# A second, channel-major copy of x in place of TensorE transposes, with the first norm's scale and shift read back as rows from DRAM

## The reference

```python
def layernorm(x):                       # over the 256 channels
    return (x - mean(x)) / sqrt(var(x) + 1e-5)
def attn(x):                            # RWKV time mixing
    x_prev = x shifted by one token
    xk, xv, xr = (x * m + x_prev * (1 - m) for m in (mix_k, mix_v, mix_r))
    k, v, r = xk @ W_k.T, xv @ W_v.T, sigmoid(xr @ W_r.T)
    return (r * wkv_scan(k, v, decay, first)) @ W_o.T      # a scan over tokens
def ffn(x):                             # ternary weights w, scales s
    h = silu(x @ w1.T * s1) * (x @ w2.T * s2)              # 256 -> 1024
    h = gelu(h @ h1.T * sh1); h = gelu(h @ h2.T * sh2)     # 1024 -> 1024, twice
    return h @ w3.T * s3                                   # 1024 -> 256
x = x + attn(layernorm(x)); x = x + ffn(layernorm(x))
```

## Time and profile before

| | |
|---|---|
| median of 3 runs | 1482.69 us (1480.98 to 1483.41) |
| the profiled execution | 1483.14 us, its span 1481.4 us |
| busy share of the span | PE 99%, PEld 90%, DVE 74%, ACT 70%, POOL 6% |
| chain that ended last | PE 98%, ACT 1%, DVE 1% |
| granted TensorE clock | 1.00 throughout |

### The profile page before, as it was taken

The page is one execution under the profiler, slowest core; times in us unless marked ns, Lnnn a source line. Parts: engine busy times, 40 slices in busy tenths (PEclk is TensorE's granted clock), DMA queues, the critical chain, the costliest instruction groups (busy, mean ns, idle before and its releaser), DMA issues.

```text
span 1481.4 us, 28040 instructions
## 1 busy us (share of the span) xinstructions
PE 1471.6 (99%) x10348; PEld 1328.8 (90%) x10348; DVE 1100.9 (74%) x1519; ACT 1040.1 (70%) x1637; POOL 93.2 (6%) x125
## 2 busy tenths in 40 slices
PE   8999999999999999999999999999999999999998
PEld 7989898998989989898898989989899898998998
DVE  6786878768687686877858777686876868778565
ACT  7995775777667676676867767776677766768655
POOL 1112000010000101001010000100001000010000
PEclk9999999999999999999999999999999999999999
DMA  9987573745737467364564746557374673746653
GB/s 353 382 293 240 171 237 104 237 131 199 233 97 252 114 205 216 124 230 135 204 184 155 229 112 228 154 179 240 100 238 120 212 220 107 250 117 205 178 191 124
DMA packets 95070, 285.28 MB, mean 193 GB/s; under 512 B 9152, under 2 KB 33344, under 8 KB 93248
## 3 DMA queue, kind: packets, MB, share of 16 engines
q1 hardware_dynamic: 86880, 277.01, 55.4%
q0 software_dynamic: 8160, 7.87, 4.3%
HBM read 250.76 MB, written 33.03 MB: 192 GB/s over the span
## 4 chain that ended last, share of the span: by engine, by line
PE 98%; ACT 1%; DVE 1%; issue 0%; POOL 0%; POOLq 0%; DVEq 0%; ACTq 0%
PE acc L674 27%; PE acc L676 26%; PE att L567 10%; PE acc L649 7%; PE acc L648 7%; PE acc L700 4%; PE acc L702 4%; PE att L606 3%; PE att L546 2%; PE acc L803 2%; PE acc L805 2%; PE att L649 1%; PE att L648 1%; PE acc L774 1%; PE acc L543 0%; ACT early L1209 0%
## 5 line engine op out<-in xcount | busy, mean ns | idle before, releaser
L674 PE MATMUL acc<-op_hi,ring 128*128 128x256 f32 x3360 | 810.9, 286 | 0.5 <-issue 0.5
L676 PE MATMUL acc<-op_lo,ring 128*128 128x256 f32 x3360 | 789.0, 278 | 0.0
L674 PEld LDWEIGHTS acc<-op_hi,ring 128*128 128x128 f32 x3360 | 632.1, 188 | 18.7 <-issue 17.6
L676 PEld LDWEIGHTS acc<-op_lo,ring 128*128 128x128 f32 x3360 | 631.1, 188 | 11.1 <-issue 10.0
L1654 DVE TENSOR_TENSOR op_lo<-blocks,op_hi 128x1024 fp32r<-128x1024 f32 (+2 forms) x271 | 339.7, 1268 | 110.7 <-ACT op_hi L1074 104.0
L1074 ACT ACTIVATE op_hi<-blocks 128x1024 fp32r<-128x1024 f32 (+2 forms) x263 | 284.1, 1092 | 81.3 <-DVE blocks L1649 75.0
L648 PE MATMUL acc<-x_hi,w_rnd 128*128 128x512 f32 x420 | 167.3, 398 | 0.0
L649 PE MATMUL acc<-x_lo,w_rnd 128*128 128x512 f32 x420 | 166.1, 396 | 0.0
L1114 ACT ACTIVATE blocks<-acc,vec 128x256 f32<-128x256 f32 x268 | 104.8, 476 | 68.3 <-PE acc L676 60.8
L1114 ACT ACTIVATE blocks<-parts,vec 128x256 f32<-128x256 f32 x240 | 101.1, 497 | 64.1 <-DVE parts L1712 61.5
L700 PE MATMUL acc<-w_rnd,op_hi 128*128 128x256 f32 x504 | 121.9, 284 | 0.0
(11 more groups left out here) (206 smaller groups left out, 1919.9 us busy)
## 6 DMA issues: line engine op xcount, KB each, us to landing
ring<-scratch SPq DMA_DIRECT2D x426, 512.0 KB, 4.2
scratch<-stage SPq DMA_DIRECT2D x11, 1024.0 KB, 12.6
stage<-in_w_ffn SPq DMA_DIRECT2D x10, 1024.0 KB, 10.6
x_in<-in_x SPq DMA_DIRECT2D x32, 256.0 KB, 4.7
out<-x_next SPq DMA_DIRECT2D x30, 256.0 KB, 4.9
out<-mix_v POOLq DMA_DIRECT2D x30, 256.0 KB, 4.3
scratch<-in_w_ffn SPq DMA_DIRECT2D x4, 1024.0 KB, 14.7
ring<-stage SPq DMA_DIRECT2D x7, 512.0 KB, 10.9
```

The source lines that it names most:

```text
L674: pe.matmul(out, act(w), act(op_hi[:, k, c, :]), start=(begins and c == 0 and m % 2 == 0), stop=False, skip_group_check=True)
L676: mm = pe.matmul(out, act(w), act(op_lo[:, k, c, :]), start=False, stop=(c == QC - 1), skip_group_check=True)
```

## The change

It affects tiles 2 to 15 (the loop's mixing).

- The host lays out a second copy of x by channel, x_T. SP loads a tile of it (load_xT, 512 KB in runs of 1 KB) into mix_r, which is free at the end of the iteration.
- DVE takes the statistics of tile i + 2 one iteration earlier, near the end of iteration i (next_statistics), and load_x moves from the end of SP's iteration to behind the 20th refill, where x_in is free.
- POOL makes scale and shift of them (next_deviation). Since in channel order each token is a column, they must lie along the row of every partition: spread_norm stores the 1024 numbers to DRAM in token order, waits for the store, and reads the 4 KB row back to all 128 partitions of norm, once transpose_x2 has read norm.
- POOL applies them: normal_x, a multiply and an add of 128x1024 each, from mix_r and norm into seq, at the head of its iteration.
- transpose_x, ln1 and copy_x leave the loop; the gate has no transposes within. carry_on, two copies of 128x4 that hand on the last token, moves from ACT to DVE, and DVE's mixing waits there for normal_x.
- On DVE lo01(1), prod(7), lo23(1) and lo45(1) stand earlier, on ACT hi23(1).

```diff
@@ SP
+            def load_xT(t):
+                sp.wait_ge(WHOLE.pe_kvr.sem, WHOLE.pe_kvr.at(t - 1))
+                stand_alone(sp, spare, t)
+                ld_xT.add(sp.dma_start(mix_r[:].rearrange("p c (n t) -> p (c n) t", n=n_seq), xT_tiles[:, :, t, :]))
+
+            def spread_norm(t):
+
+                sp.wait_ge(pool_rstd.sem, pool_rstd.at(t - 1, 1))
+                stand_alone(sp, spare, t)
+                st_norm.add(sp.dma_start(norm_rows.rearrange("a (k b p) -> p (a k) b", k=2, p=P), next_norm[:], allow_slow_non_contiguous=True))
+                sp.wait_ge(st_norm.sem, st_norm.at(t))
+                stand_alone(sp, spare, t)
+                sp.wait_ge(WHOLE.pe_x2T.sem, WHOLE.pe_x2T.at(t - 1))
+                stand_alone(sp, spare, t)
+                ld_norm.add(sp.dma_start(norm[:], norm_rows.broadcast_to([P, 2 * TILE])))
...
             with sp.Fori(1, NT - 2) as i:
-                refill(i)
-                load_x(i + 2)
+                refill(i, more_x=True)
                 keep_x1(i + 1)
+                load_xT(i + 2)
+                spread_norm(i + 2)
                 stored(i)
@@ TensorE, the loop
-                    gate(i, range(HC - 1))
-                    pe.wait_ge(dve_prod.sem, dve_prod.at(i, 3))
-                    transpose_x(WHOLE, i + 1)
-                    gate(i, [HC - 1])
+                    gate(i)
                     step(i, 0, 0)
                     step(i, 0, 1)
+                    pe.wait_ge(dve_prod.sem, dve_prod.at(i, 3))
                     project(WHOLE, i + 1, [0, 1, 2])
@@ ScalarE, the loop
                 silu(i, 4)
-                ln1(WHOLE, i + 1)
                 silu(i, 5)
                 hi01(i, 1)
                 silu(i, 6)
-                copy_x(WHOLE, i + 1)
                 hi45(i, 0)
                 silu(i, 7)
                 hi23(i, 0)
+                hi23(i, 1)
                 hi45(i, 1)
                 copy_kvr(WHOLE, i + 1, [0])
-                hi23(i, 1)
                 p1(i, 0)
@@ VectorE
+            def next_statistics(t):
+
+                dve.wait_ge(ld_x.sem, ld_x.at(t + 1))
+                statistics(WHOLE, t, x_in)
+                variance(WHOLE, t, dve_var.add, next_var, next_mean)
+
+            def carry_on(t):
+
+                link(WHOLE, dve.tensor_copy(seq[:, :, :, 0:1], carry_x[:]))
+                dve.wait_ge(pool_x.sem, pool_x.at(t))
+                settle(WHOLE, t)
+                link(WHOLE, dve.tensor_copy(carry_x[:], seq[:, :, :, SEG:SEG + 1]))
...
                 loG11(i)
+                next_statistics(t)
                 loG21(i)
@@ GpSimd
+            def next_deviation(t):
+                deviation(WHOLE, t, dve_var.sem, dve_var.at(t, 2), pool_rstd.add, (next_var, next_mean), (next_norm[:, 0, :], next_norm[:, 1, :]))
+
+            def normal_x(t):
+
+                pool.wait_ge(ld_xT.sem, ld_xT.at(t))
+                pool.wait_ge(ld_norm.sem, ld_norm.at(t))
+                stand_alone(pool, spare, t)
+                pool_x.add(pool.tensor_tensor(now, by_seq(mix_r[:]), row_scale, ALU.mult))
+                pool.wait_ge(pool_x.sem, pool_x.at(t, 1))
+                pool_x.add(pool.tensor_tensor(now, now, row_shift, ALU.add))
...
             with pool.Fori(1, NT - 1) as i:
-                tile_deviation(i + 1, 1)
+                normal_x(i + 1)
                 tile_deviation(i + 1, 2)
+                next_deviation(i + 1)
                 add_out(i)
```

More of the change, by code:

```diff
@@ L123, in __init__, with build @@
         self.dve_x2 = by_chunk("dve_x2", chunks, like and like.dve_x2)
-def build(nc, x, vectors, w_mix, w_ffn, s3, out):
+def build(nc, x, x_T, vectors, w_mix, w_ffn, s3, out):
     n_seq, T, D = x.shape
@@ L145, in build @@
     USES = HALF_STEPS // SLOTS
+    X_AFTER = 19
+    DVE_EXTRA = 6
     assert vectors.shape[1] == 5 * DC + 4 * HC and w_ffn.shape[1] == 2 * W12 + 2 * HH + W3
@@ L210, in build @@
         offset = sb("offset", [P, NB])
+        next_var = sb("next_var", [P, NB])
+        next_mean = sb("next_mean", [P, NB])
+        next_norm = sb("next_norm", [P, 2, NB])
         zeros = sb("zeros", [P, NB])
@@ L267, in build @@
         scratch = nc.dram_tensor("scratch", [2, STEPS + 1, 2, P, HALF], F32, kind="Internal").ap()
+        norm_rows = nc.dram_tensor("norm_rows", [1, 2 * TILE], F32, kind="Internal").ap()
         w_plain = nc.dram_tensor("w_plain", [P, W3], F32, kind="Internal").ap()
@@ L274, in build @@
         norm_ch = norm[:].rearrange("p (c t) -> p c t", c=DC)
+        row_scale, row_shift = (norm[:, k * TILE:(k + 1) * TILE].rearrange("p (a n t) -> p a n t", a=1, n=n_seq).broadcast_to([P, DC, n_seq, SEG])
+                                for k in range(2))
         out_tok = mix_v[:].rearrange("p c t -> p (c t)").rearrange("p (b d) -> p b d", b=NB)
@@ L334, in build @@
         WHOLE = Mixing(ctx, nc, DC, range(n_seq), HALVES, SEG, [BANK[b] for b in (6, 7, 6, 7)], by_block(norm[:]),
[L335 removed]
+                       Chain(ctx, nc, "dve_chain", 36), Chain(ctx, nc, "pool_chain", 2), ahead=1, seqs_ahead=0, like=FIRST[0])
         pe_a, pe_b, pe_half, pe_w3 = (tally(n, k) for n, k in (("pe_a", HC), ("pe_b", HC), ("pe_half", HALF_STEPS), ("pe_w3", 2)))
@@ L357, in build @@
         ld_x = tally("ld_x", n_seq, 16)
+        ld_xT = tally("ld_xT", 1, 16, ahead=-2)
+        st_norm = tally("st_norm", 1, 16, ahead=-2)
+        ld_norm = tally("ld_norm", 1, 16, ahead=-2)
+        pool_x = tally("pool_x", 2, 1, ahead=-2)
         st_out = tally("st_out", n_seq, 16, ahead=0)
@@ L425, in load_plain, with refill @@
                     sp.dma_start(flat(eighth[l]), src).then_inc(ld_eighth[l], 16)
-            def refill(i, last=False, following=WEIGHTS):
+            def refill(i, last=False, following=WEIGHTS, more_x=False):
                 for n in range(HALF_STEPS - SLOTS if last else HALF_STEPS):
@@ L430, in refill @@
                     load_ring((n + SLOTS) % HALF_STEPS, LAST_WEIGHTS if last else following if n + SLOTS >= HALF_STEPS else WEIGHTS)
+                    if more_x and n == X_AFTER:
+                        load_x(i + 2)
             def refill_plain(l, steps):
@@ L514, in _ @@
             load_x(2)
+            load_xT(2)
             refill_plain(1, range(SLOTS))
             keep_x1(1)
+            spread_norm(2)
             stored(0)
             with sp.Fori(1, NT - 2) as i:
-                refill(i)
-                load_x(i + 2)
+                refill(i, more_x=True)
                 keep_x1(i + 1)
+                load_xT(i + 2)
+                spread_norm(i + 2)
                 stored(i)
+            sp.sem_inc(ld_x.sem, 16 * n_seq)
             refill(NT - 2, following=LAST_WEIGHTS)
@@ L1871, in _ @@
             rest_x2(late_seq, 0)
-            dve.sem_inc(WHOLE.dve_chain.sem, WHOLE.dve_chain.per)
+            WHOLE.dve_chain.n = -DVE_EXTRA
+            dve.sem_inc(WHOLE.dve_chain.sem, WHOLE.dve_chain.per - DVE_EXTRA)
             dve.wait_ge(ld_x.sem, ld_x.at(1))
@@ L1942, in _ @@
                 prod(i, 5)
+                lo01(i, 1)
                 t23(i, 0)
-                lo01(i, 1)
                 prod(i, 6)
+                carry_on(t)
                 mix_difference(WHOLE, t)
@@ L1948, in _ @@
                 mix(WHOLE, t, 1)
+                prod(i, 7)
                 lo23(i, 0)
-                prod(i, 7)
+                lo23(i, 1)
                 t23(i, 1)
                 lo45(i, 0)
+                lo45(i, 1)
                 mix(WHOLE, t, 2)
-                lo45(i, 1)
-                lo23(i, 1)
                 t4(i)
@@ L2095, in _ @@
                 first_deviation(s, 3 + k)
-            pool.sem_inc(WHOLE.pool_chain.sem, WHOLE.pool_chain.per)
+            WHOLE.pool_chain.n = -1
+            pool.sem_inc(WHOLE.pool_chain.sem, WHOLE.pool_chain.per - 1)
             tile_deviation(1, 1)
@@ L2140 @@
         "x": a["attn_x"],
+        "x_T": a["attn_x"].transpose(2, 0, 1).reshape(-1, P, a["attn_x"].shape[0], a["attn_x"].shape[1]).transpose(1, 0, 2, 3).reshape(P, -1, a["attn_x"].shape[1]),
         "vectors": np.concatenate([columns(a[k]) for k in (
```

25 lines of the change are left out of this document (13 added, 12 removed).

## The result

The changed kernel takes 1515.55 us (median of 4 runs, 1514.48 to 1520.88) against 1483.01 us for the kernel before beside it: a ratio of 1.0229, 95% interval 1.0203 to 1.0255. It is slower by 2.3%, where 1477 us, a gain of 0.4%, was forecast, and it lies outside the range as well. The profiled execution took 1514.9 us.

The account below looks back on a forecast made before the run. It took TensorE, busy 99% of the span, as the bound. Transposes removed -12.2 us, first iteration +2.7, 13 x 0.3 of waits: -5.6 us, so 1477.1 against 1482.7, range 1470 to 1505.

Parts of the forecast that it names:

- the third link of the new path: The 4 KB store of scale and shift to DRAM, 1024 runs of 4 B: lands in 2.6 to 10.7 us, 5.0 taken.
- G + 5.0: G is the start of an iteration's gate; POOL was forecast to start normal_x 5.0 us after it.
- the prediction's own list: PE's wait per iteration by POOL's start after the gate's start: nothing up to 4.5 us, 0.3 at 5, 3.7 at 12.
- Rival 3: The 4-byte store is slow in itself, over 8 us, and DVE waits at carry_on: 1497 to 1522 us, chance 0.11.
- The prediction's estimate of 4.2 us: Alternative figure for the whole 4-byte store: 1.6 us for 1024 elements, from a strided transpose's cost, plus the fixed part.
- The removal: The 8 transposes in the gate cost PE 0.87 us in each of 14 places: 12.2 us, all of the gain.
- The row: Reading the row back to 128 partitions, 512 KB in runs of 4 KB: 4.2 us, 5 in a crowd.
- POOL's two instructions: normal_x's multiply and add on 1024 columns: 2.3 us each, 4.8 us with the wait between.
- POOL and DVE take turns by whole instructions: POOL and DVE instructions that read two SBUF tensors exclude each other for their whole length.
- one for one: PE is busy 99% of the span, so any new wait of PE is lost at its own length.
- The break-even at G + 5.7: The change turns slower from a PE wait of 0.73 us, if store and read together take over 9.9 us.
- The first iteration: Without lead there, POOL starts at 146.6, 10.9 us after the gate's start, and PE loses 2.7 us once.

Follow-up runs that it names:

- the 8 B runs: Changed kernel with the 1024 numbers stored in 512 runs of 8 B instead of 1024 of 4 B (row in a wrong order): 1502.14 us, 1.0128.
- the wide power: Changed kernel with DVE turning the statistics before POOL's power, which then works on 128x32, and a store in 32 runs of 128 B: 1499.91 us, 1.0115.
- The 32 B store done twice: Changed kernel with the numbers stored in 128 runs of 32 B (row in wrong order), twice, each waited for: 1486.96 us, 1.0029.
- the row read with a step: Changed kernel with the store in 128 runs of 32 B and POOL reading the row with a step of 8 numbers, in four instructions: 1488.93 us, 1.0043.
- the turned version: Changed kernel with DVE turning POOL's 128x4 results in 32x32 blocks, stored as 32 runs of 128 B in token order: 1472.13 us, 0.9921.
- the floor: Kernel before with the 8 transposes of x left out of each of the 14 loop iterations, nothing else changed: 1469.44 us, 0.9914.

## Why the prediction was wrong

**The step that failed** is the third link of the new path, as the prediction put it: "I take 5.0, towards the plain packet with few bytes, behind the tail of xT". It measured 10.7 us, the upper end of the range that the prediction had worked out just before from 64 packets at the accumulating packet's price. Nearly everything behind it follows: POOL at G + 11.3 instead of G + 5.0 (5.7 of these 6.3 us are the store), and by the prediction's own list 1.8 to 3.7 us for each iteration instead of 0.3. Rival 3 came true, with 0.11 of the chance, and its time (1497 to 1522) holds the result.

Why the plain packet was the wrong row: an engine's share of the store is 64, 32 or 8 runs, and in the first iteration, with SP's queue empty, they take 11.2, 4.6 and 1.4 us from the store's issue to the row's. From 8 to 32 runs that is 0.13 us a run, from 32 to 64 0.21: an estimate, from three runs, of 0.13 to 0.2 us for each short run, the higher figure with POOL's stores beside it. A packet of 1 KB that accumulates takes 0.13 and a plain one 0.05. I had argued that few bytes make a packet cheaper; no row said so.

That the measured 10.7 us are just the prediction's upper bound is partly luck, because the time is not spent as it had supposed. The accumulating packets keep the DMA engines busy while they take it. Those of the store don't. These are the transfers of the change in its first iteration, from 138 to 150 us (packets, MB, share of the 16 engines' time), of POOL's queue and of SP's, in which the store is:

```profile
q0 software_dynamic: 282, 0.28, 69.7%
q1 hardware_dynamic: 1063, 0.03, 4.5%
```

4.5% of 16 x 12 us are 8.6 us for 1063 packets, 8 ns each. In the profile's records the engines' own time with the short runs is almost nothing, and still the store has landed only at 149.5. What happens in between, no row shows. The Trainium skill (DMA: Bandwidth & Descriptors, § Specifications) says that a transfer of under 512 B is done as read-modify-write; a slow end of each write would fit that, and no run here shows the mechanism itself. The prediction's other rule of the Trainium skill, one descriptor per element (the same page, § Rules for kernel authors), agrees with the trace: packets of under 512 B rose from 9152 to 24160, of which the 14 stores are 14,336. The prediction's estimate of 4.2 us, from the strided transpose, was 2.5 times too low.

**Point by point, the rest:**
- The removal, 12.2 us: 12.5 in the run without transposes. Right.
- The statistics between loG11 and loG21 at no cost: loG21 starts behind 0.38 us of idle time. Right. The order of the gate alone costs 0.3 us in 1470, within the noise. next_norm at G - 4.5: measured G - 4.3.
- The row, 4.2 us: 4.0 in the change, but 6.2 where it falls beside POOL's own stores (the 8 B runs and the wide power). The allowance of 5 "for a crowd of this size" was too small there. In the change too POOL's store takes a part of the DMA engines at that time (47% of them from 887.2 to 891.2), and that row landed in 5.0.
- POOL's two instructions, 2.3 us each: 2.41 and 2.19 where nothing meets them; the 3.06 above contain DVE's instruction ahead of it. Right.
- That POOL and DVE take turns by whole instructions: lo01(1) and t23(0) of the changed kernel are late by the rest of POOL's instruction, to within 0.2 us, and the list of waits by POOL's start, made from this and DVE's timeline alone, is within 0.4 us of six runs. Right, and it is the more useful half of the prediction.
- That DVE would wait at carry_on, which rival 3 names beside the lateness: wrong for a start at G + 11.3. POOL's add is done at 897.86 and the copies come at 899.52. DVE had been held up so long itself that it could not be early. Right for a later start: DVE waits 6.1 us in the first iteration, with POOL at G + 16.6, and in 10 iterations of the run with the store ahead of xT.
- That a new wait of PE costs its own length, "one for one": too little where the clock falls behind it. In the change the falls lose 3.4 us in two iterations, with the store ahead of xT 15 in eight. The 32 B store done twice and the row read with a step, in which PE waits at most 1.5 and 1.7 us at a time, show no fall in the loop.
- The break-even at G + 5.7: the store done twice, at G + 6.2 to 6.8, is slower by 0.3%, and G + 4.3 is faster by 0.8%. Between them it was not measured.
- The first iteration: 2.7 us were foreseen with POOL at 146.6. In the turned version it starts at 146.7, and PE's longest wait there is 1.5 us; in the change it starts at 153.7, PE waits 4.2 and the iteration costs 5.8 above the floor.

What stays open: what the price of a short run is made of, how much of the 4 B store's time comes from POOL's stores beside it, and whether stores of short runs from another queue cost the same; none of this was tried.

## What to carry to other kernels

Price a small store to DRAM by the runs that an engine has to write, not by its bytes: here 1024 runs of 4 B took 10.7 us and 32 of 128 B, after a turn of 0.20 us on an engine that had idle time, about 3. Where a quantity on which the sign hangs has bounds far apart, and another kind of packet in the trace (the accumulating one) sits at the upper bound, ask what the unknown one has in common with each before choosing the lower. And an engine that is 88% idle is not free: its large instructions stop another engine for their whole length, so what counts is the moment at which they start, and one that is 2 us late can cost more than all that it relieves.
